# Layer 0 of a four-layer graph network: bulk zeroing and copy moved behind the first pass over edges, rows of constants gathered in the first scatter loop

## The reference, cut to what matters

```
def _hconv(x, W, b, src, dst):
    x = x @ W
    deg_n = segment_sum(ones, src, N_NODES); deg_e = segment_sum(ones, dst, N_HEDGES)
    Dinv = where(deg_n > 0, 1 / deg_n, 0);   Binv = where(deg_e > 0, 1 / deg_e, 0)
    he  = Binv[:, None] * segment_sum(x[src], dst, N_HEDGES)
    out = Dinv[:, None] * segment_sum(he[dst], src, N_NODES)
    return out + b
h = maximum(_layernorm(x), 0)
h = relu(_hconv(h, W1, b1, src, dst));  x = x + _hconv(h, W2, b2, src, dst)
```

## Time and profile before

| | us |
|---|---|
| median of 3 runs (lowest, highest) | 3318.11 (3316.03, 3324.59) |
| the profiled execution's own time | 3321.51 |
| its span in the trace | 3319.7 |
| mean granted TensorE clock | 0.828 of full speed |

### The profile page before, as it was taken

How to read it: one execution, slowest core, us unless ns; L and a number is a source line. 1 busy time by engine, 2 the same in 40 slices (tenths; PEclk the granted TensorE clock), 3 DMA queues, 4 the chain that set the end, 5 groups by cost and what they waited for, 6 DMA issues and landing times. The chain is left out here.

```text
span 3319.7 us, 49065 instructions
## 1 busy us (share of the span) xinstructions
PE 2144.1 (65%) x10561; PEld 1502.5 (45%) x10561; DVE 2130.9 (64%) x8721; ACT 1682.1 (51%) x4589; POOL 1599.9 (48%) x1491
## 2 busy tenths in 40 slices
PE   0267353563775878777772777777885777773665
PEld 0123242252553656666650333333444666662555
DVE  1268842332886889898875777776754444441999
ACT  0149310122886556565654988988974444440222
POOL 0130046643001788888845655655515777775000
PEclk9779677777998677676775999999997888785999
DMA  7930142244999778787855999988985555541998
GB/s 312 346 103 6 48 86 37 69 115 90 325 325 315 250 240 245 239 251 237 247 131 159 284 270 278 295 266 262 301 197 188 186 186 184 181 158 71 312 317 283
DMA packets 494699, 696.78 MB, mean 210 GB/s; under 512 B 66363, under 2 KB 357398, under 8 KB 485932
## 3 DMA queue, kind: packets, MB, share of 16 engines
q1 hardware_dynamic: 414254, 485.35, 47.1%
q0 software_dynamic: 63360, 130.75, 14.8%
q10 hardware_dynamic: 16896, 78.91, 6.3%
HBM read 394.91 MB, written 327.18 MB: 218 GB/s over the span
## 5 line engine op out<-in xcount | busy, mean ns | idle before, releaser
L262 POOL DMA_INDIRECT xs<-x_d,table_src x400 | 385.2, 963 | 379.4 <-DVE x L1485 148.2
L262 POOL DMA_INDIRECT xs<-n_d,srcI x200 | 234.6, 1173 | 326.3 <-DVEq L1134 270.8
L262 POOL DMA_INDIRECT xd<-n_d,dstI x200 | 239.6, 1198 | 61.0 <-issue 54.9
L262 POOL DMA_INDIRECT xd<-x_d,table_dst x200 | 211.0, 1055 | 65.1 <-issue 65.1
L1699 POOL DMA_INDIRECT r_d<-rd,out_row x200 | 196.8, 984 | 61.3 <-issue 59.1
L1640 PE MATMUL bank<-nmsg,same 128*128 128x128 f32 x400 | 100.6, 335 | 149.7 <-ACT sums L1572 92.5
L1640 PEld LDWEIGHTS bank<-nmsg,same 128*128 128x128 f32 x400 | 61.8, 195 | 286.2 <-ACT sums L1572 223.1
L1822 PE MATMUL bank<-xs,same 128*128 128x129 f32 x400 | 106.4, 355 | 129.1 <-DVE same L1764 68.3
L518 PE MATMUL bank<-mask,h 128*128 128x512 f32 x160 | 104.1, 810 | 131.8 <-DVE mask L856 79.5
L452 POOL DMA_INDIRECT sum_d<-add,to x40 | 63.7, 1593 | 240.5 <-ACT add L647 226.9
L238 DVE RECIPROCAL rs<-root 128x4 f32<-128x4 f32 (+3 forms) x253 | 51.8, 205 | 193.0 <-ACT root L257 178.6
(11 more groups left out here) (382 smaller groups left out, 7173.8 us busy)
## 6 DMA issues: line engine op xcount, KB each, us to landing
n_d<-T SPq DMA_DIRECT2D x98, 528.0 KB, 3.8
nt<-n_d SPq DMA_DIRECT2D x49, 1056.0 KB, 7.0
r<-r_d SPq DMA_DIRECT2D x98, 520.0 KB, 5.5
bc<-dst_d SPq DMA_DIRECT2D x170, 256.0 KB, 4.8
r_d<-nv SPq DMA_DIRECT2D x49, 528.0 KB, 8.1
v_d<-nv SPq DMA_DIRECT2D x49, 528.0 KB, 7.8
nv<-v_d SPq DMA_DIRECT2D x49, 528.0 KB, 4.1
x_d<-x SPq DMA_DIRECT2D x100, 256.0 KB, 4.0
```

The source lines that it names most:

```text
L262: pool.indirect_dma_start(out=out, out_offset=None, in_=table, in_offset=bass.IndirectOffsetOnAxis(ap=index, axis=0)).then_inc(s, 16)
```

## The change

The 15 zeroing DMAs go from ACT's start to SP's queue, behind the first pass's last store of `sumT` and ahead of the store of `meta_d`. The 13 copies of x go, still on ACT's queue, behind the first pass and ahead of the rest of the histogram. The gathers of `meta_d` go from the second pass to the first scatter loop: after a group's four scatters are issued, POOL copies the group's `srcI` columns to `ix`, gathers four times into `ms`, waits for the landing, copies the four rows of eight constants to the new tile `ms_all` (128 x 200 x 8) and waits for that, all before it waits for the scatters and counts `landed`. POOL therefore waits for `meta_out` ahead of the first scatter loop. The second pass and the second scatter loop read their scalars from `ms_all`; DVE's copy `dinv` is gone.

```diff
@@ sync, stages(conv)
                         lagged(sp, n, load_bc, store_sums)
                         if conv == 0:
+                            zero_rows = combine[:, :, :, :].rearrange("p s k e -> p (s k e)")
+                            sp.wait_ge(zero_ready, 2)
+                            for k in range(NN // (P * 28)):
+                                sp.dma_start(sum1_d[k * P * 28:(k + 1) * P * 28, :].rearrange("(p r) f -> p (r f)", p=P),
+                                              zero_rows[:, 0:28 * D]).then_inc(zeroed, 16)
+                            sp.dma_start(sum1_d[NN:NN + G * P, :].rearrange("(p r) f -> p (r f)", p=P), zero_rows[:, 0:G * D]).then_inc(
+                                zeroed, 16)
                             sp.wait_ge(meta_ready, 1)
@@ gpsimd, stages(conv)
                                 gather(pool, er[:, s, j, :], t["x"] if conv == 0 else sum1_d, ix[:, s, j:j + 1], er_in[conv][s])
-                                if conv == 1:
-                                    gather(pool, ms[:, s, j, :], meta_d, ix[:, s, j:j + 1], ms_in[s])
-                        if conv == 1:
-                            pool.wait_ge(meta_out, 16)
                         bounded(pool, n, gathers)
                         if conv == 0:
                             pool.wait_ge(zeroed, 16 * (NN // (P * 28) + 1))
+                            pool.wait_ge(meta_out, 16)
@@ gpsimd, scatter(g, s)
                                                         compute_op=ALU.add).then_inc(e["added"], 16)
+                            if conv == 0:
+                                nc.gpsimd.tensor_copy(ix[:, s, :], srcI[:, bass.ds(g * G, G)]).then_inc(e["mx_ready"], 1)
+                                hold("pool", pool, e["mx_ready"], g + 1)
+                                for j in range(G):
+                                    gather(pool, ms[:, s, j, :], meta_d, ix[:, s, j:j + 1], ms_in[s])
+                                hold("pool", pool, ms_in[s], pre_count(g, s, G))
+                                nc.gpsimd.tensor_copy(ms_all[:, bass.ds(g * G, G), :], ms[:, s, :, :]).then_inc(ms_ready, 1)
+                                hold("pool", pool, ms_ready, g + 1)
                             pool.wait_ge(e["added"], g * (16 * G) + 16 * G)
                             pool.sem_inc(e["landed"], 1)
@@ scalar
                     act.wait_ge(zero_ready, 2)
-                    (the 15 zeroing DMAs and the 13 copies, L580 to L588)
                     act.wait_ge(groups_ready, 1)
@@ scalar, stages(conv)
                         lagged(act, n, relus, sums)
                         if conv == 0:
+                            for k in range(NX // COPY):
+                                act.dma_start(x1_d[k * COPY:(k + 1) * COPY, :].rearrange("(p r) f -> p (r f)", p=P),
+                                              t["x"][k * COPY:(k + 1) * COPY, :].rearrange("(p r) f -> p (r f)", p=P)).then_inc(x_copied, 16)
                             bounded_from(act, n, NH, signs)
@@ vector, first_sums(g, s)
-                            dve.wait_ge(ms_in[s], pre_count(g, s, G))
-                            nc.vector.tensor_copy(dinv[:, bass.ds(g * G, G)], ms[:, s, :, M_DINV])
+                            dve.wait_ge(ms_ready, g + 1)
-                                    ... scalar=ms[:, s, j, M_DINV:M_DINV + 1],
+                                    ... scalar=ms_all[:, bass.ds(g * G + j, 1), M_DINV],
```

More of the change, by code:

```diff
@@ L317, in build @@
             ms = sb("ms", [P, 2, G, 8], F32, c)
-            dinv = sb("dinv", [P, NT], F32, c)
+            ms_all = sb("ms_all", [P, NT, 8], F32, c)
             last_cols = sb("last_cols", [P, 2 * G], F32, c)
@@ L328, in build @@
             ms_in = [sem(f"ms_in{s}") for s in range(2)]
+            ms_ready = sem("ms_ready")
             q = [{n: sem(f"c{conv}_{n}") for n in (
-                "ix_ready", "stats_link", "mixed", "rooted", "inverted", "scaled", "row_link", "h_ready", "mask_ready",
+                "ix_ready", "mx_ready", "stats_link", "mixed", "rooted", "inverted", "scaled", "row_link", "h_ready", "mask_ready",
                 "sums_ps", "sums_in", "across_ps", "across_in", "reach_ready", "he_ps", "count_link", "binv_ready", "he_ready",
@@ L579, in _ @@
                     act.wait_ge(zero_ready, 2)
[L580 to L588, removed]
                     act.wait_ge(groups_ready, 1)
@@ L651, in additions @@
                                     last = nc.scalar.activation(add[:, s, j, :], comb_bank[s][:, j * P:(j + 1) * P], ACT.Copy,
-                                                                scale=dinv[:, bass.ds(g * G + j, 1)])
+                                                                scale=ms_all[:, bass.ds(g * G + j, 1), M_DINV])
                             last.then_inc(e["add_ready"], 1)
@@ L825, in first_sums @@
                         def first_sums(g, s):
-                            dve.wait_ge(ms_in[s], pre_count(g, s, G))
-                            nc.vector.tensor_copy(dinv[:, bass.ds(g * G, G)], ms[:, s, :, M_DINV])
+                            dve.wait_ge(ms_ready, g + 1)
                             for j in range(G):
                                 last = nc.vector.scalar_tensor_tensor(
-                                    out=er[:, s, j, :], in0=er[:, s, j, :], scalar=ms[:, s, j, M_DINV:M_DINV + 1],
+                                    out=er[:, s, j, :], in0=er[:, s, j, :], scalar=ms_all[:, bass.ds(g * G + j, 1), M_DINV],
                                     in1=R["b1"][:, :], op0=ALU.mult, op1=ALU.add)
@@ L835, in first_sums @@
                                 last = nc.vector.scalar_tensor_tensor(
-                                    out=er[:, s, j, :], in0=he_last[0][:, :], scalar=ms[:, s, j, M_CHIGH:M_CHIGH + 1],
+                                    out=er[:, s, j, :], in0=he_last[0][:, :], scalar=ms_all[:, bass.ds(g * G + j, 1), M_CHIGH],
                                     in1=er[:, s, j, :], op0=ALU.mult, op1=ALU.add)
```

## The result

The changed kernel takes 3216.65 us (median of 4 runs, 3215.13 to 3221.78), the kernel before in the same session 3317.07 (4 runs, 3309.16 to 3324.59): a ratio of 0.9692 with a 95% interval of 0.9668 to 0.9715. The profiled execution has a span of 3213.3 us, where before it was 3319.7. The forecast was 3265 with a range of 3238 to 3306: the direction held, the size did not. The gain is 100 us where 53 were forecast.

The account below looks back on a forecast made before the run. Bound: layer 0's serial chain, its start held by bulk DMA while compute engines are nearly idle. Terms -102 + 33 + 5 + 56 - 45 = -53 us, against 3318.1, give 3265; the 8-in-10 range is 3238 to 3306.

Parts of the forecast that it names:

- part 1: Layer 0's start: with bulk transfers moved out, the first pass's relu 9 comes at 146.8 instead of 248.81; -102 us.
- part 2: Histogram tail: ACT's 13 copy issues ahead of its signs lie wholly on the path; +33 us, between 19 and 49.
- My lower bound of 19 us: Histogram tail: 13 undisturbed copy issues on ACT, at the earlier median of 1.45 us each, would take 19 us.
- the rival of a shared generator: Histogram tail: ACT's copies each wait for one SP zeroing issue; stall 49 us instead of 33, time 3281; chance 0.22.
- the throttled issues: Histogram tail: ACT's copies wait behind throttled zeroings; stall 132 us instead of 33, time 3364, slower than before; chance 0.08.
- part 3: Histogram tail and finalize: zeroing and copy running underneath delay them little; +5 us, bounds 0 and 30.
- The cover of 35 us: After finalize: bulk ends near 300 us, zeroed rows are first needed at 335, so the wait is covered by 35.
- part 4: First scatter loop: gathers of constants lengthen the closed chain by 5.6 us for each of ten groups; +56 us.
- The rival that the gathers would hide in the landings: First scatter loop: gathers of constants cost nothing on the path; 56 us less, time 3209; chance 0.05.
- part 5: Layer 0's second pass without the gathers of constants: steps of 6.6 us instead of 11.04, group 0 earlier; -45 us.

Follow-up runs that it names:

- `swapped`: The changed kernel with the 15 zeroings issued by ACT and the 13 copies of x by SP; 3585.6 us, one run, on a slower chip.
- `gathers_only`: The kernel before with only the gathers of constants moved, zeroing and copies staying at ACT's start; 3607.15 us, ratio 1.0052.
- `after_filler`: The changed kernel with 15 one-column activations added at ACT's start, in the place of the 15 removed issues; 3234.66 us, ratio 0.9762.
- `before_filler`: The kernel before with 24 one-column activations on ACT ahead of its zeroing; 3575.38 us, ratio 0.9991.
- `small_copies`: The changed kernel with the copy of x cut into 52 DMAs of 0.5 MB instead of 13 of 2.1 MB; 3242.21 us, one run.

## Why the prediction was too small

**The start (part 1) was right.** Relu 0 came at 55.68 (56.5 forecast) and relu 9 at 144.95 (146.8): 103.9 us where 102 was said.

**The failed step is part 2, ACT's copy issues: 33 us forecast, 8.5 measured.** I had taken the undisturbed price from the earlier trace rows, where the median copy took 1.45 us, and added for SP. But those 13 stood in ACT's queue right behind 15 zeroings, and their 1.45 was already a disturbed price: each takes 0.61 us (median) when no zeroing stands before it in its own queue, in every run that has the copies on ACT behind the first pass. No run issued them at the start without the zeroings, so that it is the queue, and not the place in time, is argued from the two prices. My lower bound of 19 us was therefore no bound. SP's zeroing hardly touched them (607 to 678 ns, the last four of them at 612 to 623 inside an issue of 11.7 us), so the rival of a shared generator (49 us) fell further than the forecast, and the throttled issues (132 us) fell with it. Throttling does exist: it hits the queue of the zeroing itself, and `swapped` shows the 94 us that it costs there.

The Trainium skill's page "Perfetto Trace Analysis", section "DMA Instruction — HWDGE (DVE, Sync)", whose lock on a shared descriptor generator I had weighed, isn't borne out as a lock that lasts for a whole long issue: ACT's four issues inside SP's of 11.7 us show nothing of it. In the kernel before, SP's `first_d` issue at 44.57 us, which took 0.29, already lay inside a zeroing issue of ACT of 4.19 us (41.71 to 45.91). A disturbance by short issues does exist in one direction: in `swapped`, SP's copies took 0.84 to 1.46 us (median 1.33) beside ACT's zeroings of 0.84 to 1.30, and 0.59 after them. Which part the two share is open.

**The tail (part 3): 5 forecast.** From relu 9 to the end of finalize took 161.6 us, 11.7 more than before; 8.5 is the copies, about 3 the rest. The bulk ended at 295 (near 300 forecast), 7 us ahead of the store of `meta_d` and 12 ahead of `across`. The cover of 35 us was counted from a finalize end at 335; with the end at 306.55 it shrank to 12, which still suffices.

**The first scatter loop (part 4): +56 forecast, +60.8 measured.** The chain is closed as described, and rounds are 18.8 to 19.4 us against 18.2. POOL's index copy took 0.78 us instead of the 0.18 of the earlier trace rows; that is most of the difference. The rival that the gathers would hide in the landings is refuted by `gathers_only`. **The second pass (part 5): -45 forecast, -48.3 measured**, with steps of (578.3 - 520.9) / 9 = 6.4 us where 6.6 was said. Together the two parts lose: +12.5 in the changed kernel, +10.4 in `gathers_only`. The forecast had +11.

**What no step named: layer 2, -17.4 us.** This is the second step that failed: I read what layer 0 gains as what the kernel gains, and took the stages behind it as fixed, at a difference of 0. Taking 15 instructions out of ACT's code ahead of them moved all that follows, and the idle time before `hsT` fell. `after_filler` and `before_filler` show this from both sides in the profiles of the stage; in the time of the kernel the first shows it weakly and the second not. What mechanism makes one place better than another is open: the fetch queue's packets don't follow it. The other 11 us outside layer 0 are mostly the attention stage of layer 1 (698.3 to 690.9); over the kernels with the changed start on the first chip it lay between 688.8 and 698.0 us (the last in `small_copies`), so all of it may be spread. No run separates it.

The sum in the profile: 25 us of the missing 53 are part 2 (33 - 8.5), 28 the later stages; parts 1, 3, 4 and 5 cancel to about 2.

## What to carry to other kernels

A bulk transfer's cost to its issuer is read only from issues with no other kind of bulk before them in their queue; put the kind that is held back on an engine for which nobody waits, and test it by swapping the two. Work added to a closed round between engines costs its full length; count the hand-over first and do the rest behind it (3221 to 3190 us here, 25 us of it in the loop). And where a change adds or removes instructions ahead of later loops, keep some 20 us open for those loops, or test with fillers.

## What the runs showed of the hardware that was not expected

- A copy from memory to memory takes its issuer 0.61 us (median), for 2.1 as for 0.5 MB, and 1.45 behind zeroings in the same queue. A zeroing of 1.8 MB from the on-chip tile takes 0.33 us at best and 27.2 at worst; 15 in sum, beside the copies, take 106 us on SP and 102 on ACT.
- An issue of 11.7 us on SP left the issues of ACT inside it at 0.61 us. Short zeroing issues of ACT (0.84 to 1.30 us) raised SP's copies from 0.59 to a median of 1.33.
- 52 smaller copies shortened SP's 14 zeroing issues from 102.21 to 55.41 us in sum. Why was not tried.
- Moving ACT's code by 15 or 24 instructions changed a stage of 720 to 790 us by 15 to 20 us, mostly in idle time before a few instructions (0 to 12.1 us in sum at `hsT` in the short form, 19.1 to 27.7 in the long), with the activations as long as before.
